# A decoder layer on one core: one key tile's penalties as a product on VectorE for batches 1 to 3, and both ends of the kernel rearranged

## What is computed

```
g = sigmoid(x @ Wg + bg);  Z_I, Z_J = g, swapaxes(g, 1, 2)
res = (1 - Z_I) * maximum(1 - Z_I - Z_J, 0) + Z_I * minimum(1 - Z_I + Z_J, 1)
scope = clip(power(s - 2, 1 - g) + 2 - abs(i - j), 1e-32, 1)
penalties = res * scope
scores = q k^T / 4 + log(maximum(penalties, 1e-32))        # self-attention
x = layernorm(x + softmax(scores) v)
x = layernorm(x + (softmax(q k^T / 4 + mask * -1e9) v) @ Wo + bo)   # k, v from the context
xq = fake_quant(x);  h = silu(xq @ Wgate^T) * (xq @ Wup^T)
out = layernorm(x + fake_quant(h) @ Wdown^T)
```

## Time and profile before

| | |
|---|---|
| median of 3 runs | 812.96 us (811.87 to 818.21) |
| the profiled execution's own time | 813.62 us |
| its span in the profile | 811.8 us |
| instructions | 10697 |
| mean granted TensorE clock | 0.937 of full |

### The profile page before, as it was taken

How to read it: one execution, slowest core, us unless ns; L and a number is a source line. 1 busy time by engine, 2 the same in 40 slices (tenths; PEclk the granted TensorE clock), 3 DMA queues, 4 the chain that set the end, 5 groups by cost and what they waited for, 6 DMA issues and landing times.

```text
span 811.8 us, 10697 instructions
## 1 busy us (share of the span) xinstructions
PE 665.3 (82%) x3350; PEld 267.6 (33%) x3350; DVE 611.4 (75%) x1576; ACT 482.0 (59%) x800; POOL 328.8 (41%) x417
## 2 busy tenths in 40 slices
PE   6178878999889899998899899989889899838562
PEld 3043223533322243343232443433222242224231
DVE  3988984687799876686997566569786969348996
ACT  3214647556546868654478687446667667816444
POOL 6204855656466314645663034566413001001314
PEclk9668999999999999999999899999999999987865
DMA  2550352230411432321204213422414210000002
GB/s 91 154 141 25 101 124 70 67 68 21 122 45 45 114 69 72 87 72 42 66 29 123 49 51 99 104 55 86 94 30 113 68 41 4 3 1 0 2 0 103
DMA packets 34888, 53.85 MB, mean 66 GB/s; under 512 B 4369, under 2 KB 25873, under 8 KB 34833
## 3 DMA queue, kind: packets, MB, share of 16 engines
q1 hardware_dynamic: 32912, 51.61, 23.7%
q10 hardware_dynamic: 1920, 1.57, 1.2%
HBM read 36.91 MB, written 14.68 MB: 64 GB/s over the span
## 4 chain that ended last, share of the span: by engine, by line
PE 41%; DVE 25%; POOL 12%; ACT 9%; issue 8%; DMA 4%; SPq 0%; ACTq 0%; POOLq 0%; DVEq 0%
PE ps L1484 9%; POOL probs L687 8%; PE ps L1460 8%; PE ps L1440 7%; DVE dist L968 6%; PE ps L1427 5%; PE ps L1343 4%; ACT probs L872 4%; DMA QS<-mT 3%; PE ps L1420 2%; PE ps L1464 1%; PE ps L1465 1%; DVE x L1005 1%; POOL parts L718 1%; DVE pen_a L1031 1%
## 5 line engine op out<-in xcount | busy, mean ns | idle before, releaser
L1440 PE MATMUL ps<-KS,QS 96*128 96x512 bf16 x512 | 199.0, 392 | 42.8 <-DVE mx L968 28.2
L872 ACT ACTIVATE probs<-ps 128x512 f32<-128x512 f32 x256 | 149.1, 596 | 123.8 <-PE ps L1465 90.6
L1460 PE MATMUL ps<-QS,KS 108*128 108x512 bf16 x512 | 197.6, 386 | 23.0 <-ACT probs L872 13.9
L968 DVE CUSTOM_DVE_ANT_0 dist<-ps,lp 128x512 bf16<-128x512 f32 x256 | 169.6, 685 | 61.5 <-PE ps L1440 56.3
L687 POOL TENSOR_TENSOR probs<-probs,penT 128x512 f32<-128x512 f32 x128 | 169.3, 1343 | 112.9 <-ACT probs L872 112.9
L872 ACT ACTIVATE probs<-ps,mask_col 128x512 f32<-128x512 f32 x256 | 167.2, 690 | 50.0 <-PE ps L1460 46.9
L968 DVE CUSTOM_DVE_ANT_0 dist<-ps,mask_rest 128x512 bf16<-128x512 f32 x192 | 126.5, 684 | 30.9 <-PE ps L1440 30.8
L1440 PEld LDWEIGHTS ps<-KS,QS 96*128 96x128 bf16 x512 | 50.7, 99 | 189.7 <-DVE mx L968 118.2
L1460 PEld LDWEIGHTS ps<-QS,KS 108*128 108x128 bf16 x512 | 50.2, 98 | 103.2 <-ACT probs L872 63.9
L1484 PE MATMUL ps<-probs,v_s 128*32 128x512 f32 x512 | 68.8, 609 | 15.9 <-POOL probs L687 15.9
L1484 PE MATMUL ps<-probs,v_c 128*32 128x512 f32 x512 | 68.2, 604 | 0.9 <-ACT probs L872 0.9
(11 more groups left out here) (186 smaller groups left out, 946.6 us busy)
## 6 DMA issues: line engine op xcount, KB each, us to landing
parts_qs<-parts SPq DMA_DIRECT2D x8, 384.0 KB, 2.5
parts_ks<-parts SPq DMA_DIRECT2D x8, 384.0 KB, 2.5
KS<-parts_ks SPq DMA_DIRECT2D x16, 192.0 KB
QS<-parts_qs SPq DMA_DIRECT2D x16, 192.0 KB
parts_kc<-parts SPq DMA_DIRECT2D x8, 384.0 KB, 2.5
KS<-parts_kc SPq DMA_DIRECT2D x16, 192.0 KB
parts_qc<-parts SPq DMA_DIRECT2D x8, 384.0 KB, 2.5
QS<-parts_qc SPq DMA_DIRECT2D x16, 192.0 KB
```

The lines of the kernel that those rows point to most:

```text
L872: s_.activation(probs[:, T % NP, :], ps[:, EXP_BANKS[T % len(EXP_BANKS)], :], ACT.Exp, bias=bias)\
L968: v.tensor_tensor_reduce(out=unused[:, (TG * n + i) % AHEAD, :], in0=ps[:, MAX_BANKS[(TG * n + i) % AHEAD], :], in1=lp[:, t, :] if kind == ...
L1440: mm(ps[:, MAX_BANKS[(TG * n + i) % AHEAD], :], QS[0:SK, slot, j, t * P:(t + 1) * P], KS[0:SK, slot, j, :], start=True, stop=True).then_in ...
L1460: ins = mm(o, KS[0:SM, slot, j, kt * P:(kt + 1) * P], QS[0:SM, slot, j, :], start=True, stop=not logged)
```

## The change

**Key tile 1 in batches 1 to 3.** `by_vector(b, kt)` is true for kt 1 and b from 1. There the two log products on TensorE are left out, `lpB` writes the transposed penalties into a third tile of `penT`, and a job `penalise` on VectorE multiplies the four exponential tiles, three slots behind. The context product of that key tile waits for VectorE and stands in slot 3 in place of slot 2. Batch 0 keeps the logs.

**Gates.** The gate jobs of batches 1, 2 and 3 are spread over more slots.

**Start.** `own_rows` moves ahead of the prologue on VectorE, `gate` 1 and `reach` ahead of the first k projection, and a first exp on a constant loads ScalarE's table at the start.

**End of attention.** The last exponential tiles use three banks in place of two; the first half of the last output projection (feature chunk 0, row tiles 0 and 1) is done while the exponentials run; its results are added row tile by row tile from four banks (`last_x1`). The sigmoid of the clips moves ahead. `whole_max` loses two copies and one wait, at both of its places.

**Down projection.** The rounding of blocks 1 and 2 moves from VectorE to ScalarE (`rounded`); block 3 is rounded on VectorE right after block 1 is clipped. The first block's products start as soon as a group of its integers is clipped. GpSimd's addition for block 0 goes to VectorE. The last block is scaled, added and measured in halves, and normalised on VectorE in place of ScalarE.

```diff
+VEC_KT, VEC_FROM = 1, 1
-DVE_LATE = {"norm": 3, "v": 3, "wo": 3, "lpB": 3}
+DVE_LATE = {"norm": 3, "v": 3, "wo": 3, "lpB": 3, "penalise": 3}
...
+        for slot in range(TG):
+            e = s.exp_at(slot)
+            if e and groups[e[0]][0] == "s" and by_vector(groups[e[0]][1], e[1] // GH):
+                s.items[slot].append(("penalise", *e))
...
-    add(("s", 0, 1), stacks=[], fetch=[("keys", 0), ("cT", 0)], tasks=[(0, 5, ("gate", 1)), (4, 15, ("q", "s", 1)), (7, 15, ("pens", 1, (0,)))])
+    add(("s", 0, 1), stacks=[], fetch=[("keys", 0), ("cT", 0)], tasks=[(0, 8, ("gate", 1)), (4, 15, ("q", "s", 1)), (7, 15, ("pens", 1, (0,)))])
...
-    add(("s", 1, 3), at=[(15, ("mask_col",))], tasks=[(1, 6, ("q", "c", 0)), (7, 8, ("mask", 0)), (8, 14, ("gate", 2))])
+    add(("s", 1, 3), at=[(15, ("mask_col",))], tasks=[(1, 6, ("q", "c", 0)), (7, 8, ("mask", 0)), (3, 14, ("gate", 2))])
...
-    add(tasks=[(0, 8, ("wo", B - 1)), (9, 9, ("ln2", B - 1))])
+    add(at=[(5, ("c2T", B - 1, 0)), (9, ("first_half", B - 1))], tasks=[(2, 15, ("wprep", 2))])
+    add(at=[(2, ("sigmoids",))])
+    add(at=[(0, ("c2T", B - 1, 1)), (1, ("second_half", B - 1))]
+        + [(2, ("last_x1", B - 1, t)) for t in range(NT)] + [(3, ("x2stats", B - 1, t)) for t in range(NT)],
+        tasks=[(4, 4, ("ln2", B - 1))])
...
+        DRAIN_T, DRAIN_BANKS, WO_BANKS = TG * (len(groups) - 2) + TG // 2, (3, 4, 0), (1, 2, 0, 3)
...
+            def rounded(tc):
+
+                for lo, hi in H_GROUPS:
+                    m, cols = ISZ[lo], slice(tc * 512, (tc + 1) * 512)
+                    s_.activation(h_all[0:m, lo:hi, cols], h_all[0:m, lo:hi, cols], ACT.Copy, bias=MAGIC,
+                                  scale=scal[0:m, 8:9]).then_inc(h_rounded, 1)
...
+                elif what == "penalise":
+                    n, i = job[1:]
+                    T, b = TG * n + i, groups[n][1]
+                    if groups[n][2] == 0 and i % GH == 0:
+
+                        used(dve, unit[("lpB", b, VEC_KT)])
+                    dve.wait_ge(exp_done, T + 1)
+                    v.tensor_tensor(probs[:, T % NP, :], probs[:, T % NP, :], penT[:, len(MUL_KT), :], ALU.mult)\
+                        .then_inc(pen_by_vector, 1)
...
-                logged = kind == "s" and kt not in MUL_KT
+                logged = kind == "s" and kt not in MUL_KT and not by_vector(b, kt)
...
+                elif kind == "s" and by_vector(b, kt):
+                    pe.wait_ge(pen_by_vector, by_vector_until(n))
...
-                        if e[1] % GH == 2 and e[1] > GH:
+                        kind, b, _ = groups[e[0]]
+                        late = kind == "s" and by_vector(b, e[1] // GH - 1)
+                        if e[1] % GH == (3 if late else 2) and e[1] > GH:
```

More of the change, by code:

```diff
@@ L61, with by_vector @@
 STACK_DMAS = 2 * PARTS
+def by_vector(b, kt):
+    return b >= VEC_FROM and kt == VEC_KT
 class Step:
@@ L439, in logs, with by_vector_until, kept @@
         def logs(b, kt):
-            return len(log_kt) * b + log_kt.index(kt) + 1
+            return [(i, k) for i in range(b + 1) for k in log_kt if not by_vector(i, k)].index((b, kt)) + 1
+        def by_vector_until(n):
+            return GH * sum(kind == "s" and by_vector(b, VEC_KT) for kind, b, _ in groups[:n + 1])
+        def kept(b, kt):
+            return MUL_KT.index(kt) if kt in MUL_KT else len(MUL_KT)
         def multiplied(n, kt):
@@ L851, in do @@
                     s_.activation(oT[:, :], ps[:, PV_BANK, :], ACT.Copy).then_inc(o_copied, 1)
+                elif what == "sigmoids":
+                    act.wait_ge(loaded["masks"], 16 * 2)
+                    s_.activation(sig[:, :], clips[:, :], ACT.Exp, scale=-1.0).then_inc(f_exp, 1)
                 elif what == "wturn":
@@ L1196, in _ @@
             link(v.scalar_tensor_tensor(neg_abs[:, :], neg_abs[:, :], -1.0, neg_abs[:, :], ALU.mult, ALU.min))
+            dve.wait_ge(loaded["gate"], 16 * 3)
+            v.tensor_scalar(bg[:, :], bg[:, :], -1.0, None, ALU.mult).then_inc(gate_ready, 1)
+            dve.wait_ge(consts, 5 + PARTS)
+            v.tensor_copy(KS[SK:SK + VC, :, :, :].rearrange("p r j n -> p j r n"),
+                          own_rows[:, :].unsqueeze(2).unsqueeze(3).broadcast_to((VC, GH, RING, S)))\
+                .then_inc(own_rows_made, 1)
             dve.wait_ge(loaded["qk"], 16 * 3)
@@ L1312, in _ @@
                 for t in range(NT):
-                    statistics(rows, t)
+                    statistics(y[:, tc, :, :], t)
+            round_h()
+            clip_h(1)
+            for lo, hi in H_GROUPS:
+                h = h_all[0:ISZ[lo], lo:hi, (TC - 1) * 512:TC * 512]
+                v.tensor_scalar(h, h, scal[0:ISZ[lo], 8:9], MAGIC, ALU.mult, ALU.add).then_inc(last_h_rounded, 1)
+            dve.wait_ge(h_scale_made, 1)
+            for tc in range(TC - 1):
+                if tc:
+                    leave(scale_rows(tc))
+                else:
+                    scale_rows(0).then_inc(y_scaled, 1)
+                if tc + 2 < TC:
+                    clip_h(tc + 2)
+                if tc:
+                    settle()
+                else:
+                    dve.wait_ge(y_scaled, 1)
+                row_statistics(tc)
+            dve.wait_ge(var_made, 2 * B + TC - 1)
+            dve.wait_ge(y_made, TC - 2)
+            for half in range(2):
+                tiles = slice(half * NT // 2, (half + 1) * NT // 2)
+                dve.wait_ge(down_full, TC + half)
+                rows = y[:, TC - 1, tiles, :]
+                link(v.tensor_tensor(rows, ps[:, DOWN_BANKS[TC - 1] + half, :].rearrange("p (b n) -> p b n", b=2),
+                                     out_row[:, :].unsqueeze(1).broadcast_to((P, NT // 2, H)), ALU.mult))
+                link(v.tensor_tensor(rows, rows, x2[:, NT * (TC - 1) + 2 * half:NT * (TC - 1) + 2 * half + 2, :], ALU.add))
+                for t in range(2 * half, 2 * half + 2):
+                    statistics(y[:, TC - 1, :, :], t)
+            for t in range(NT):
+                normal(y[:, TC - 1, t, :], y[:, TC - 1, t, :], t, last_y_made)
         @block.tensor
```

193 lines of the change are left out of this document (113 added, 80 removed).

## The result

| | before | after |
|---|---|---|
| median | 812.64 us (811.87 to 818.21, 4 runs) | 829.43 us (826.71 to 833.48, 4 runs) |
| profiled execution, its span | 813.62, 811.8 us | 833.48, 831.6 us |
| mean granted TensorE clock | 0.937 | 0.899 |

The ratio is 1.0196, 95% interval 1.0133 to 1.0259: the changed kernel is 1.3 to 2.6% slower. I had forecast 805.7 us and a range of 793 to 815. All medians here are over every execution; without those that lie over 1.5% above the fastest of their version, e1 would stand at 807.5 us, e2 at 822.0, e13 at 801.2, e14 at 818.7, and the others where they are.

The account below looks back on a forecast made before the run. No engine is full; the bound varies by stage: VectorE in starved stretches, GpSimd's chain ahead of slot 14's context product elsewhere. Ends -15.2 plus middle +7.9 made -7.3 us, so 805.7 us against 812.96, range 793 to 815.

Parts of the forecast that it names:

- Removed: the log products: TensorE in key tile 1, batches 1 to 3: 96 products fewer, -5.3 us, bounds 0 and -21.
- GpSimd's chain: Self-attention steps outside the starved stretches: VectorE's products lengthen GpSimd's work that the slot 14 context product awaits, +6.3 us.
- Added: 48 products on VectorE: Key tile 1, batches 1 to 3: the multiplications on VectorE cost +12.4 and +6.3, together +18.7 us.
- starved stretch: Where batch penalties are made, VectorE has no idle time and TensorE waits; 18 products of 0.69 us cost +12.4.
- the meetings: VectorE's and GpSimd's products exclude each other: two in (s, 2, 1), one in eight other steps, 0.69 us each.
- Gates: Spreading the gate jobs over more slots saves 4.5 us in (s, 1, 3) and 1.0 in (s, 0, 1).
- Start: Prologue: earlier reach and no own_rows copy in between bring the first row maximum from 43.78 to 39.8, -4.0 us.
- End of attention: Last output projection, sigmoid and whole_max links get shorter: -2.8 us, bounds -2 to -3.6.
- the drain's -1.5: Last exponentials of attention: a third bank saves some of ScalarE's idle time, -1.5 us, bounds 0 to -2.5.
- the second whole_max: Second place of whole_max, with copies and a wait removed: -0.6 us.
- Down projection: After the second whole_max: VectorE relieved of roundings, clip and normalisation changes, -6.3 us, bounds -4 and -7.5.
- The product queue decides: Rival for the VectorE products: each costs 0.8 us on the path beside GpSimd, giving 825 us; chance 0.10.

Follow-up runs that it names:

- e1: Changed kernel with key tile 1's log products back on TensorE in every batch, no products on VectorE; 808.0 us, ratio 0.992.
- e2: Changed kernel with the fetch of batch 1's xT issued right after the stack of group 1; 822.8 us, ratio 1.011.
- e13: e10 with the gate of batch 3 spread over slots 0 to 6 as before; 802.4 us, ratio interval 0.977 to 0.991.
- e14: e8 with own_rows copied on ScalarE, plus products on VectorE and no logs for key tile 1 of batches 1 to 3; 818.8 us, ratio 1.007.
- e5: Changed kernel with the edits of e1 and e2 together: ends and gates only, earlier transfer; 796.5 us, ratio 0.979.
- e10: e2 with neither log products nor VectorE products in key tile 1 of batches 1 to 3, context product in slot 2; 805.5 us.
- e6: e2 with each VectorE product cut to one column of 128, waits and order kept; 805.3 us, ratio 0.990.
- e4: Changed kernel with TensorE's log products of key tile 1 kept beside the VectorE products; 833.9 us, ratio 1.025.
- e15: e8 with own_rows copied on ScalarE and the gate of batch 2 back over slots 8 to 14; 798.6 us.
- e8: e5 with the gate of batch 3 spread over slots 0 to 6 as before; 794.3 us, ratio interval 0.973 to 0.978.
- e16: e8 with own_rows copied on ScalarE and, in batch 1 alone, products on VectorE in place of logs; 798.4 us.
- e9: e6 with TensorE's log products of key tile 1 kept, as in e4; 805.8 us, ratio interval 0.989 to 0.996.

## Why the prediction was wrong

By medians, in the order e5, e10, e2, changed kernel, the account is: ends and gates 796.5 - 812.6 = -16.1; logs removed 805.5 - 796.5 = **+9.0**; products added 822.8 - 805.5 = **+17.3**; the late transfer 829.4 - 822.8 = **+6.6**. Together +16.8, the result. Mine was -20.7, -5.3, +18.7 and nothing: -7.3. Of the 24.1 us between the two, 14.3 are the log term, 6.6 the transfer and 4.6 ends and gates, less 1.4 for the products. Two steps failed in kind: that work removed ahead of a wait can't cost time, and that the start's edit moves nothing but what it names.

- **"Removed: the log products", -5.3.** Wrong in sign. I had the mechanism half right: TensorE's work ahead of the context product is worth next to nothing, since GpSimd's chain releases it. I bounded the term by 0 on the side of loss. But the removed work kept TensorE busy through that wait; e10 shows that without it the waits grow and the clock is at 1.2 GHz for 51 us more in the span. Since e6, e10 and e13 all show the loss with VectorE's products small or absent, it is TensorE's. The longer waits and the fall of the clock behind them stand in four steps of all three profiles; the profiles place 7.3 us (e10) and 9.2 us (e13) behind the first missing product. That every us of it goes by way of the clock is argued, not shown.
- **"Added: 48 products on VectorE", +18.7.** Measured +17.3; their time alone 17.5 (e6). The forecast of the starved stretch (41.2 to near 46; it is 45.7) and its reason (VectorE full, e4) hold. But that the sum came close is partly luck. In the two stretches of the earlier trace rows the changed kernel is 9.2 us longer than e10 (I had 14 x 0.69 = 9.7). GpSimd's chain, which I put at +6.3, gives little: in the self-attention steps from (s, 1, 1) on the waits of the context products for GpSimd add up to 15.5 us in e10 and 17.8 in e2, so +2.3; in (s, 2, 1) the wait goes from 2.81 to 3.70 us, in (s, 2, 3) it is 3.12 in both. What fills the gap I had not counted: (s, 3, 3), for one, is 3.9 us longer than in e10 (27.4 for 23.5). Steps (s, 2, 2) and (s, 2, 3), where the penalties of batch 3 begin, I had not counted among the starved ones; the changed kernel loses 6.4 us there, partly by the moved gate. Nor do the meetings show where I looked for them: GpSimd's 128 products take 169.3 us in all before and after, while VectorE's take 42.3 for 48, 9.5 more than at the median of 683 ns. 17 of the 48 take over 1 us; of the first products of each four, 8 of 12 overlap one of GpSimd's. The later place of the context product and VectorE's waits cost nothing without the logs (e6 and e10 differ by 0.2 us).
- **"Gates", -5.5.** Step (s, 1, 3) gives 3.1 us; e15's 8.7 would make it worth more, but no row shows where. The wait of 0.93 us in (s, 0, 1) I can't tell from the transfer's effect. The gate of batch 3, which I treated as the same jobs taken earlier, costs 2.2 us by the step's length (e8): it pushed `reach` into the slot where the penalties begin.
- **"Start", -4.0.** The first row maximum came at 40.39 (forecast 39.8). The step that failed is the account of the edit itself: I followed `own_rows`, `gate` 1 and `reach` on VectorE, ScalarE and TensorE, and not the k projection that they overtake. Its parts are stored by SyncE, whose stack loads wait for the stores, and the fetch of `xT` waits behind these. It cost 6.6 us here and costs 11.5 without the products (e1 and e5).
- **"End of attention", -2.8 with the drain's -1.5, "the second whole_max" -0.6, "Down projection" -6.3.** Sum -11.2. In e5 the time behind the last max tile is 11.1 us shorter; behind the second `whole_max` it was 42.7 and is 36.7 us, forecast 36.4. In the changed kernel's profile the sum is 8.1, with 48.8 us at half clock for e5's 39.3. The same tail takes 113.0 to 116.1 us in the profiles of e2 to e16, so the agreement of 11.1 with my 11.2 is the better end of a scatter of 3 us.
- **The rivals.** "The product queue decides" came near in microseconds (825) but not in kind: products cost 0.36 us each on the path (17.3 / 48; I had 0.39), not 0.8. None of my cases had a loss from the removed work, or one from a transfer.

What stays open: e9, with all the logs and products of one column, should by the clock theory stand near e5 and stands 9.3 us above it. VectorE's 48 waits and the later context product cost something when the logs are there and nothing when they are not. In its profile 4.1 us of it lie in step (s, 1, 3), where the clock falls with TensorE hardly waiting; why it does so there I don't know.
